# Graph layers on one core: TensorE signals through a drain behind the last matmul instead of from the matmul itself

## The reference

```python
def layer0(h): # neighbour mean
    s = segment_sum(h[src], dst); c = segment_sum(1, dst)
    return concat([h, s / clip(c, 1)]) @ W.T + b
def layer1(h): # a gate for each edge
    theta = h[dst] - h[src]
    w = sigmoid(relu(theta @ W1 + b1) @ W2 + b2)
    return segment_sum(w * theta, dst) + indeg * (h @ W4 + b4)
def layer2(h): # neighbour mean of a projection, ELU, row norm
    p = relu(h @ Wp.T + bp)
    o = elu(segment_sum(p[src], dst) / max(c, 1) @ Wl.T + bl + h @ Wr.T)
    return h + o / max(norm(o), 1e-12)
def layer3(h): # a weight matrix for each edge type
    msg = einsum('ni,rio->rno', h, weight)[etypes, src] * norm
    return segment_sum(msg, dst) + h @ loop_weight
```

## Time and profile before

| | us |
|---|---|
| median of three runs | 6219.24 |
| the profiled execution, own time | 6220.82 |
| its span | 6218.9 |
| PE busy / POOL busy / DVE busy | 3862.1 / 3717.9 / 2875.8 |
| layer 0 | 0 to about 1197 |
| layer 1, its gathers | 1197.2 to 3465.8 (first and last start) |
| layer 2 | about 3561 to 4160 |
| layer 3, its gathers of `tab_rel` | 4344.1 to 6204.5 (first and last start) |

### The profile page before, as it was taken

The page is one execution under the profiler, slowest core; times in us unless marked ns, Lnnn a source line. Parts: engine busy times, 40 slices in busy tenths (PEclk is TensorE's granted clock), DMA queues, the critical chain, the costliest instruction groups (busy, mean ns, idle before and its releaser), DMA issues.

```text
span 6218.9 us, 69225 instructions
## 1 busy us (share of the span) xinstructions
PE 3862.1 (62%) x20719; PEld 2994.6 (48%) x20719; DVE 2875.8 (46%) x9736; ACT 1423.7 (23%) x5476; POOL 3717.9 (60%) x3922
## 2 busy tenths in 40 slices
PE   4888888665555555555555488867466655665433
PEld 3445555554444444455555366644344444454332
DVE  7776666555444555555555533343332222222222
ACT  5333333332222233333333301122000000000000
POOL 4234444266666666666666466645666666666665
PEclk7799999777767777777777799988777777777666
DMA  3233333444444444444444455545111111111121
GB/s 108 83 112 117 127 136 136 128 138 135 141 136 135 140 140 137 146 140 139 139 147 142 135 189 202 200 158 188 45 46 46 46 46 46 47 45 47 46 63 48
DMA packets 310271, 707.07 MB, mean 114 GB/s; under 512 B 72640, under 2 KB 155292, under 8 KB 297612
## 3 DMA queue, kind: packets, MB, share of 16 engines
q0 software_dynamic: 159184, 377.89, 21.5%
q1 hardware_dynamic: 148700, 323.81, 15.0%
q10 hardware_dynamic: 2016, 0.92, 0.1%
HBM read 571.29 MB, written 131.05 MB: 113 GB/s over the span
## 4 chain that ended last, share of the span: by engine, by line
PE 32%; another core or an unknown queue 28%; DVE 21%; issue 15%; ACT 3%; DVEq 1%; SPq 1%; DMA 0%; POOL 0%; ACTq 0%
PE ps L2577 11%; DVE oneh L1866 7%; PE ps L2533 4%; PE ps L2562 3%; DVE ps L2001 3%; PE ps L2472 2%; PE ps L2484 2%; PE ps L2600 2%; PE ps L2540 2%; DVE third L1993 2%; DVE turned_words L1958 2%; DVE tmp L1957 1%; PE ps L2422 1%; PE ps L2536 1%
## 5 line engine op out<-in xcount | busy, mean ns | idle before, releaser
L1473 POOL DMA_INDIRECT rows<-tab_rel,third x1299 | 1250.3, 963 | 626.4 <-issue 369.4
L1473 POOL DMA_INDIRECT rows<-tab_hp,idx_src x1120 | 1084.2, 968 | 556.5 <-issue 307.7
L1473 POOL DMA_INDIRECT rows<-tab_h,idx_src x810 | 779.3, 962 | 857.5 <-PE ps L2540 517.1
L2600 PE MATMUL ps<-third 128*128 128x128 f32 x3126 | 612.1, 356 | 676.5 <-issue 383.5
L2577 PE MATMUL ps<-third,h 128*120 128x385 bf16 (+20 forms) x4606 | 866.4, 335 | 55.4 <-DMA h<-cnt_d 23.0
L2600 PEld LDWEIGHTS ps<-third 128*128 128x128 f32 x3126 | 546.1, 261 | 731.2 <-issue 421.7
L2533 PE MATMUL ps<-oneh,rows 128*128 128x128 f32 x2598 | 476.6, 336 | 565.0 <-issue 297.2
L2533 PEld LDWEIGHTS ps<-oneh,rows 128*128 128x128 f32 x2598 | 426.3, 243 | 640.3 <-issue 342.3
L1684 ACT ACTIVATE turned_words<-turned_words 128x128 f32<-128x128 f32 x1563 | 462.9, 297 | 1101.6 <-DVE turned_words L2006 857.8
L2577 PEld LDWEIGHTS ps<-third,h 128*120 128x120 bf16 (+10 forms) x4606 | 587.3, 131 | 265.5 <-issue 40.6
L1473 POOL DMA_INDIRECT third<-tab_hp,idx_src x443 | 428.4, 967 | 217.6 <-issue 122.4
(11 more groups left out here) (279 smaller groups left out, 4920.3 us busy)
## 6 DMA issues: line engine op xcount, KB each, us to landing
third<-dst_flat SPq DMA_DIRECT2D x390, 256.0 KB
h<-cnt_d SPq DMA_DIRECT2D x48, 1568.0 KB
cnt_d<-h SPq DMA_DIRECT2D x46, 1568.0 KB
tab_rel<-third SPq DMA_DIRECT2D x49, 512.0 KB
rows<-tab_rel,third POOLq DMA_INDIRECT x1299
rows<-tab_hp,idx_src POOLq DMA_INDIRECT x1120
rows<-tab_h,idx_src POOLq DMA_INDIRECT x810
third<-tab_hp,idx_src POOLq DMA_INDIRECT x443
```

Of the source, the lines that this page charges most:

```text
L1473: pool.indirect_dma_start(out=to[:, t, 0:n], out_offset=None, in_=table[:, :], in_offset=bass.IndirectOffsetOnAxis(ap=idx[:, col:col + 1], ...
L2600: last = pe.matmul(ps_t[sl][:, t * P:(t + 1) * P], onehT[:, sl, t * P:(t + 1) * P], pwin[:, st["v"] % 2, :], start=True, stop=True)
```

## The change

Nine kinds of PE step no longer raise their semaphore from the last matmul. They issue a `drain` behind it, and the drain raises the semaphore. The kinds are `scatter`, `scatter_h`, `expand`, `far_turn`, `rels_h`, `count3`, `mult3`, `rels3`, `put3`. `count`, `pack_mm`, `pack_turn`, `turn`, `self_mm`, `p_mm`, `m_mm`, `rel`, `sums`, `post_mm` and the steps of the preparation keep their signals on the matmul. No wait, value, order, buffer or operand changes on any engine.

```diff
                 elif kind == "count3":
-                    last.then_inc(s_count3.handle, 1)
+                    pe.drain().then_inc(s_count3.handle, 1)
...
                 elif kind == "mult3":
                     if q1 == nb:
-                        last.then_inc(s_mult3.handle, 1)
+                        pe.drain().then_inc(s_mult3.handle, 1)
...
                 elif kind == "rels3":
-                    last.then_inc(s_rels3.handle, 1)
+                    pe.drain().then_inc(s_rels3.handle, 1)
...
                 elif kind == "put3":
-                    pe.matmul(ps[4][:, 2 * P:2 * P + WIN], out3[0:n, :], place[0:n, st["u"] % 2, 0:WIN], start=True, stop=True
-                              ).then_inc(s_put3.handle, 1)
+                    pe.matmul(ps[4][:, 2 * P:2 * P + WIN], out3[0:n, :], place[0:n, st["u"] % 2, 0:WIN], start=True, stop=True)
+                    pe.drain().then_inc(s_put3.handle, 1)
...
                 elif kind == "scatter_h":
-                    last.then_inc(s_scat.handle, 1)
+                    pe.drain().then_inc(s_scat.handle, 1)
...
                 elif kind == "rels_h":
-                    last.then_inc(s_hrel.handle, 1)
+                    pe.drain().then_inc(s_hrel.handle, 1)
...
                 elif kind == "scatter":
-                    last.then_inc(s_scat.handle, 1)
+                    pe.drain().then_inc(s_scat.handle, 1)
...
                 elif kind == "far_turn":
-                    last.then_inc(s_gturn.handle, 1)
+                    pe.drain().then_inc(s_gturn.handle, 1)
...
                 elif kind == "expand":
-                    last.then_inc(s_expand.handle, 1)
+                    pe.drain().then_inc(s_expand.handle, 1)
```

## The result

The changed kernel takes 6423.78 us (median of 4 runs, 6414.76 to 6428.60) against 6219.91 for the kernel before beside it: a ratio of 1.0328, with a 95% interval of 1.0315 to 1.0341. The profiled execution took 6414.76 us, its span is 6413.0.

A forecast was written before the change was run, and what follows sets the result against it. The prediction took POOL's gathers plus 509 us of pauses for late PE signals to bound layers 1 and 3, PE layers 0 and 2. 6220.8 - 380 (prompt signals) + 20 (drains) = 5860 us, range 5715 to 6340.

The forecast's parts named there:

- the term of -380 us: Layers 1 and 3, heads and stretches between: prompt drain signals remove most POOL pauses, -380 us (0 to -509).
- What bounds the kernel: POOL's gathers set a floor in layers 1 and 3, with pauses on top; PE is full in layers 0 and 2.
- the 509 us: POOL's pauses on top of its gather floor: 296 us in layer 1, 156 and 57 in layer 3.
- The first rival: Every group: the drain waits for whatever holds the matmul's signal and PE stands; +1670 us, some 7890 us, chance 0.14.
- The second rival: Drain's signal is held like the matmul's, but PE isn't; pauses stay, drains cost 20 to 130 us; 6290 us, chance 0.11.
- The third: Signals aren't late, the trace is: a modelled end hides late matmuls; 6220 to 6230 us, chance 0.05.
- the fourth: Signals prompt, but PE becomes the bound: layer 3's dense stretch gains nothing, layers 0 and 2 lose 60; 6000 us.
- What a drain costs PE: Each of some 1660 drains takes 0.25 us of PE, at most 0.5; prices sum to +20 us (0 to +70).
- the cover: Drain costs hidden by POOL's floor in layers 1 and 3, and partly in layer 0 by POOL's gathers.
- Layer 2's term: Layer 2: drains cost another 15 us, against some gain from prompt slots; net 5 us.
- Layers 1 and 3 at nothing: Drains of 196 us in layer 1 and 108 in layer 3's long stretch fit PE's idle time, priced at nothing.
- What would show it wrong: POOL pauses once a group with PE idle until then (first rival), or "remote" wait sums stand as before (second).

The follow-up runs named there:

- the bench: Separate kernel, nothing of the reference computed: PE groups of four fp32 matmuls and a drain; DVE's longest wait 22.3 us beside back-to-back gathers, 2.3 to 3.0 otherwise.
- The run with both: Changed kernel with the signal back on the last matmul and a non-signalling drain behind it, in all nine kinds: 1.0337 of the kernel before, 6485.18 us.
- the pair: Kernel before and changed kernel, both with two waited-for 64-column POOL memsets behind each gather of layers 1 and 3, chip without hold: 6857.47 and 6926.93 us.
- The doubled expansions: Kernel before with each expansion matmul of layer 1 issued twice, on chips without the hold: 1.0002 and, repeated, 0.9999 of the kernel before.

## Why the prediction was wrong

**The step that failed** is "I take prompt as likelier, not as shown": the term of -380 us. The drain's signal does not go round the held completions; it comes when they have come, 20.8 us behind a group's start in layer 3 of the changed kernel, and up to 22.3 us in the bench, as late as a matmul's. The run with both (1.0337) shows that moving the signal brought nothing at all. In place of -380 us the change cost 204. Its reason was a leap: DVE's signals cross at once in the earlier trace rows, so what is held belongs to PE's matmuls, "and once the array is empty its own signal need not queue with theirs". The first half was right. But an array whose completions aren't delivered isn't idle to a drain: the bench's drains last 2.8 us for each matmul instruction before them.

**What bounds the kernel** was read rightly. Without the hold, layer 1's gathers take 1980.5 for 2268.6 us, layer 3's 1642.4 for 1860.4 (5535.6 - 3893.2), and the kernel 5550 us. The pauses were sized well, 288 + 218 us by these rows, if the two chips differ in the hold alone, which no run proves. What the 509 us left out is layer 2 and the heads, which were held too: from the last gather of layer 1 to the first of layer 3 it is 730.1 us (3893.2 - 3163.1) against 878.3 in the kernel before. Nothing in the earlier trace rows could tell that of a stage in which PE is busy.

**The first rival** had the mechanism and missed the size eightfold, +204 us for +1670. It took the hold as a delay that each signal pays in full, 5.07 + 2.5 us a group. The bench shows a rate instead, 2.8 us for each matmul instruction once it has built up. A PE that stands sends nothing more into what is held, which would make the next hold shorter, and the rows agree: DVE's waits of layer 1 doubled in number, 151 to 286, and halved in length, 4.5 to 2.5 us. Its condition, a hold over 1.3 us of idle time a drain, did name the right side. Its counter-argument, that PE goes on running while signals are out, is what gave it 0.14, and the bench refutes it once the hold has built up: 16 matmul instructions in 45 us.

**The second rival** (6290 us, signal held, PE not) is the nearest in time and wrong in kind: PE is held. **The third** (the trace is late, not the signals) falls with the 22.3 us of the bench, and **the fourth** with the first term.

**What a drain costs PE** was priced at 0.25 us, and the price was right: 0.27 in layer 0, 0.34 in the idle bench. Wrong was the cover. Layer 0 was to lose 15 of 33 us and lost 35.9, on either kind of chip: at 88% busy nothing was hidden. Layer 2's term, 15 less a gain of 10, came out at 25.7. Layers 1 and 3 at nothing is shown right only where nothing is held and the gathers are spaced (1 us and 0); where completions are held, they carry 77.9 + 38.5 + 10.0 of the 194 us.

**What would show it wrong** named what came: PE idle behind its groups. The sum of waits stood as before, which was the second rival's mark; the two rivals' marks should have been told apart by PE's "issue" rows, 371.4 us in 374 waits before scatters (L2536, layer 1) against 117.2 in 170 in the kernel before.

**Still open:** what the queue is that gathers and PE's completions share; whether it counts a matmul, its weight load or both; whether it is a matter of the chip or of what else ran beside it; what the changed kernel takes, unspaced, on a chip without the hold (from the pair, its layers 0 and 2 would cost 69 us; layers 1 and 3 are not measured there at 1.25 us). So a share of their loss that is the drains' own cost, at the full pace of the gathers, is not ruled out. Each timed execution left a record of its span and clock; whether recording has a part in the hold was not tried. The doubled expansions were not run on a chip that holds.

## What to carry to other kernels

A drain's signal came no earlier here than the last matmul's, and the engine can't run meanwhile; where a signal is late, keep it on the matmul and find what makes it late. Before a latency is multiplied by a count, ask whether it is a delay or a rate: a bench with one, two and four times the work per wait tells them apart. And where a resource is at its limit, a pause moved from one engine to another isn't a pause saved: compare the rate over the stage with the one at which the bench came free.

## What the runs showed of the hardware

- Beside back-to-back indirect gathers on POOL (one per 1.25 us), PE completes one matmul instruction per 2.8 us, with a drain or without. Drains grow past 2.5 us within 2 to 16 us of a phase's start and reach the full length after 21 to 41. Gathers of 16 rows or of 16 columns do the same; direct loads by SP or POOL and memsets don't (longest wait 3.0 us).
- It is gone between 1.44 and 1.49 us a gather, beside groups of four fp32 matmuls.
- Of the five chips of the experiments two show nothing of it, and the same kernel takes 5550 and 5558 us there for 6218 to 6271 elsewhere: 11 per cent, three times what the change moves. One chip gave 6267 us at one time and 6221 at another. Only kernels run beside each other on one chip can be compared.
- A drain behind four fp32 matmuls costs PE 0.34 us with nothing beside it (1.23 for 0.89 us a group), and 0.27 us in layer 0 of the kernel.
